# TensorE's reads of expert numbers in the routed loops of layers 1 and 2: four checked reads for a pair of tiles, or one read of three at the head

## The chip, the cores and the metric

The kernel runs on one core of a Trainium2 chip, in one launch. The metric is the device time of that launch in microseconds. Times "from the span's start" count from the first instruction of the profiled execution.
## What is computed

Four transformer layers, each a cross-attention and then a mixture of eight experts, of which every token uses two. Layers 1 and 2 are the ones that the change touches:

```python
# layer 1: 2048 tokens, D = 256, hidden 512, top 2 of 8, and a shared expert
h1 = einsum('td,edh->eth', xf, w1);  h3 = einsum('td,edh->eth', xf, w3)
y  = einsum('eth,ehd->etd', silu(h1) * h3, w2)
out = einsum('etd,te->td', y, cw) + silu(xf @ sw1) * (xf @ sw3) @ sw2
# layer 2: hidden 1024, top 2 of 8
h = gelu(einsum('nd,edf->enf', u, W1) + b1)
out = einsum('ne,end->nd', gates, einsum('enf,efd->end', h, W2) + b2)
```

The kernel computes an expert only for the tokens that chose it.

## The kernel before

**Routing.** The router's choice is turned into a list of slots: tokens that chose the same expert stand together, in tiles of 128 rows. 2048 tokens with two choices each, and up to 7 partly filled tiles, make SLOT_TILES = 39 tiles. VectorE writes two small tables in `vector_tables` (L504): `table`, the expert of each tile, clamped to 7 where it is made (L522), and `rows`, where the tile's rows lie in memory. The tables hold 42 entries of int32 on one partition.

**The routed loop.** `routed_layer` (L1871) is used for layers 1 (swiglu, hidden 512) and 2 (gelu, hidden 1024). All weights of the eight experts are resident in SBUF, so choosing an expert is choosing an address. Each engine has its own program, and `each_pair` (L1945) makes it go over the 39 tiles in pairs: tiles 0 and 1 are written out, then a hardware loop `Fori(1, 19)` runs 18 times with two tiles in its body (2i and 2i + 1, u = 0 and 1), and tile 38 is written out behind it. The loop's own steps (count, compare and branch, copy of the index) are recorded at L1948.

**TensorE's order for tile j** (the body at L2106):

- L2109 and L2110 wait for the rows of tile j + 1 to be in SBUF and for the turned rows of tile j to be copied out; `turn_rows` (L2087, matmuls at L2090) transposes the rows of tile j + 1;
- L2113 and L2114 read from `table` the expert of tile j and that of tile j - 1, each by `expert_of` (L2100, one value a read, with a check of its bounds while running; the records stand at L2101);
- the first product (L2120) of tile j with w1 and w3 of its expert (layer 1), or with two halves of w1 (layer 2): four matmuls of 512 columns, each recorded as two passes, so 8 records a tile;
- the second product (`output`, L2093, matmuls at L2096) of tile j - 1 with w2 of *its* expert: 8 records a tile in layer 1, 16 in layer 2;
- the transposes (L2132) of the hidden values of tile j, which wait (L2128) until they are there.

So four reads are made for a pair of tiles, of three different entries: 2i - 1, 2i (twice) and 2i + 1. After the loop the expert of the last tile is read once more (L2137).

**Around it.** VectorE copies the turned rows to SBUF (L2245), makes the hidden values (layer 1: L2272, silu times the second half; layer 2: it adds the bias at L2267 and ScalarE applies gelu at L2171), copies the output (L2253, L2255) and the turned hidden values (L2277). SyncE loads the rows of tile j + 2 (L1981) and stores the output of tile j - 1 (L2008); in layer 2 it loads bias rows too, and has checked reads of its own (L1963, L1978). None of these programs is touched. The block ends with a barrier of all engines, and the next layer's attention begins behind it.

**The same read elsewhere.** Layer 0's loop (`routed_half_layer`, written out, with no hardware loop) already reads two entries at once, without a check (`experts_of`, L2453, recorded at L2454).

Of the kernel before, what the change touches and what calls it, by code (L numbers as in the profile page):

```python
# [28 lines left out]
E = 8  # L29
# [1841 lines left out]
def routed_layer(nc, kept, cfg, route, resident, w, slots_in, slots_out, pre_next):  # L1871
# [15 lines left out]
    NT = SLOT_TILES  # L1887
    LAST = len(cfg.choose_groups) - 1
    COUNT_AT = D

    ctx = ExitStack()
    with ctx:
# [9 lines left out]
        ident, table = kept.ident, route.table  # L1902
# [42 lines left out]
        def each_pair(engine, body):  # L1945

            body(0, 2)
            with engine.Fori(1, NT // 2) as i:  # L1948
                body(i, 2)
            body(NT // 2, NT % 2)  # L1950
# [80 lines left out]
        @block.tensor  # L2031
        def _(pe):
            def shared_first(n):
                g, m = divmod(n, M)
                if n >= 2:
                    pe.wait_ge(sh_ready, n - 1)
                for bank, weight in zip(banks[2 * (m % 2):2 * (m % 2) + 2], (sw1, sw3)):
                    for k in range(DK):
                        last = nc.tensor.matmul(bank[:, 0:GN], weight[:, k, m * P:(m + 1) * P],
                                                route.xT[:, k, g * GN:(g + 1) * GN], start=(k == 0), stop=(k == DK - 1))  # L2040
                last.then_inc(sh_full, 1)

            def shared_second(g):
                for m in range(M):
                    pe.wait_ge(sh_ready, g * M + m + 1)
                    if m == 0 and g > 0:
                        pe.wait_ge(sy_out, g * GT)
                    for t in range(GT):
                        last = nc.tensor.matmul(banks[4 + t][:, 0:D], shT[:, m, t * P:(t + 1) * P], sw2[:, m, :],
                                                start=(m == 0), stop=(m == M - 1))  # L2050
                        if m == M - 1:
                            last.then_inc(sy_full, 1)

            def shared_expert():
                shared_first(0)
                shared_first(1)
                route.tensor_turn(pe, banks[4], BATCH - 1).then_inc(turned_full, 1)
                shared_first(2)
                pe.wait_ge(turned, 1)
                route.tensor_logits(banks[5], BATCH - 1).then_inc(logits_full, 1)  # L2060
                shared_first(3)
                pe.wait_ge(route.logged, 1)
                shared_second(0)
                shared_first(4)
                shared_first(5)
                pe.wait_ge(sy_out, GT)
                route.tensor_count(pe, count_bank, LAST, COUNT_AT).then_inc(counted, 1)
                shared_first(6)
                shared_first(7)
                pe.wait_ge(count_out, 1)  # L2070
                shared_second(1)
                for g in range(2, NG):
                    for m in range(M):
                        shared_first(g * M + m)
                    shared_second(g)

            if cfg.shared:
                pe.wait_ge(resident.shared_in, 48)
                shared_expert()
                pe.wait_ge(sy_out, TILES)  # L2080
            else:
                route.tensor_count(pe, count_bank, LAST, COUNT_AT).then_inc(counted, 1)
                pe.wait_ge(count_out, 1)
            pe.wait_ge(route.tabled, 1)
            pe.wait_ge(resident.landed, resident.total)

            def turn_rows(u):  # L2087

                for k in range(DK):
                    last = nc.tensor.transpose(a_bank[:, k * P:(k + 1) * P], xg[u][:, k * P:(k + 1) * P], ident[:, :])  # L2090
                last.then_inc(a_full, 1)

            def output(e, u):  # L2093

                for m in range(M):
                    last = nc.tensor.matmul(d_bank[:, 0:D], hT[u][:, m, :], resident.second[:, bass.ds(e, 1), m, :],  # L2096
                                            start=(m == 0), stop=(m == M - 1))
                last.then_inc(d_full, 1)

            def expert_of(j):  # L2100
                return nc.tensor.value_load(table[0:1, bass.ds(j, 1)], min_val=0, max_val=E - 1)  # L2101

            pe.wait_ge(xg_in[0], 16)
            turn_rows(0)

            def body(i, tiles):  # L2106
                for u in range(tiles):
                    j = 2 * i + u
                    pe.wait_ge(xg_in[1 - u], 16 * (i + 1 + u))  # L2109
                    pe.wait_ge(a_out, j + 1)  # L2110
                    turn_rows(1 - u)
                    first = isinstance(i, int) and i + u == 0
                    e = expert_of(j)  # L2113
                    e_before = None if first else expert_of(j - 1)  # L2114
                    pe.wait_ge(h_done, CREDIT + HD * j)
                    for c in range(NB):
                        for k in range(DK):
                            weight = resident.firsts[c if swiglu else 0]
                            cols = slice(0, 512) if swiglu else slice(c * 512, (c + 1) * 512)
                            last = nc.tensor.matmul(b_banks[c][:, :], xgT[u][:, k, :], weight[:, bass.ds(e, 1), k, cols],  # L2120
                                                    start=(k == 0), stop=(k == DK - 1))
                        last.then_inc(b_full, 1)
                    if not first:
                        pe.wait_ge(c_out, CREDIT + HC * j)
                        pe.wait_ge(d_out, CREDIT + j - 1)
                        output(e_before, 1 - u)
                    for c in range(HC):
                        pe.wait_ge(h_done, CREDIT + HD * j + (c + 1 if gelu else 1))  # L2128
                        if c == 0:
                            pe.wait_ge(c_out, CREDIT + HC * j)  # L2130
                        for m in range(4):
                            last = nc.tensor.transpose(c_banks[c][:, m * P:(m + 1) * P],  # L2132
                                                       h[:, (4 * c + m) * P:(4 * c + m + 1) * P], ident[:, :])
                        last.then_inc(c_full, 1)

            each_pair(pe, body)
            e_last = expert_of(NT - 1)  # L2137
            pe.wait_ge(c_out, CREDIT + HC * NT)
            pe.wait_ge(d_out, CREDIT + NT - 1)
            output(e_last, (NT - 1) % 2)  # L2140
# [37 lines left out]
        def _(dve):  # L2178
# [28 lines left out]
            if cfg.shared:  # L2207
# [12 lines left out]
                dve.wait_ge(counted, 1)  # L2220
                route.vector_slots(step, count_bank, LAST, COUNT_AT)
                route.vector_totals(step, count_bank, COUNT_AT)
                dve.sem_inc(count_out, 1)
# [9 lines left out]
            else:  # L2233
                route.vector_ask(dve, step, LAST)
                route.vector_choose(dve, step, LAST)
                dve.wait_ge(counted, 1)
                route.vector_slots(step, count_bank, LAST, COUNT_AT)
                route.vector_totals(step, count_bank, COUNT_AT)
                dve.sem_inc(count_out, 1)
# [736 lines left out]
def build(nc, ap, x_out):  # L2976
# [17 lines left out]
    for n in range(4):  # L2994
        experts, w = EXPERTS[n], weights(f"f{n}_")
        rows_in, rows_out = (half_in, half_out) if n == 0 else (slots_in, slots_out)
        with ExitStack() as held:
# [25 lines left out]
            if n == 0:  # L3023
                routed_half_layer(nc, kept, experts, route, resident, w, rows_in, rows_out, ahead[n + 1], ap["ctx"])
            elif n < 3:
                routed_layer(nc, kept, experts, route, resident, w, rows_in, rows_out, ahead[n + 1])
            else:
                dense_layer(nc, kept, experts, route, resident, x_out, w)
# [17 lines left out]
```

## Time and profile before

| what | us |
|---|---|
| median of 3 runs | 2201.01 (2200.44 to 2202.23) |
| the profiled execution, whole | 2198.09 |
| its span, first to last instruction | 2196.3 |
| around the span | 1.8 |
| layer 1's routed loop, first L2120 of tile 0 to that of tile 38 | 808.40 to 1055.00 |
| layer 2's routed loop, the same | 1271.95 to 1576.17 |
| PE busy over the whole span | 1955.2 (89%) |

### The profile page before, as it was taken

The page shows a single profiled execution, that of the slowest core. Times are in us where ns is not written, and L with a number is a line of the kernel's source. Part 1 is how long each engine was busy: PE and PEld are TensorE (multiplying, and loading weights), DVE is VectorE, ACT ScalarE, POOL GpSimd, SP SyncE. Part 2 cuts the span into 40 slices and gives each one's busy share as a digit, 9 for nine tenths or more (in the row PEclk, how much of TensorE's full clock was granted, in tenths as well). Part 3 has the DMA queues.
Part 4 walks back from the last instruction along what each step waited for, and adds up shares of the span by engine and source line. Part 5 has one row for each costly group of instructions (what it writes and reads, how often), then busy time and mean ns, then how long its engine had stood idle before and what let it go on. Part 6 is the DMA issues. An engine that isn't in the chain of part 4 may idle for free. (4 is left out here: it accounts for less than half of the span.)

```text
span 2196.3 us, 30936 instructions
## 1 busy us (share of the span) xinstructions
PE 1955.2 (89%) x9735; PEld 1309.1 (60%) x9736; DVE 1221.0 (56%) x3287; ACT 710.1 (32%) x1593; POOL 223.8 (10%) x237
## 2 busy tenths in 40 slices
PE   4999889889987999999797389999969999999999
PEld 3666555557765655555575356777635666655665
DVE  3878885557777423333356634444326766667553
ACT  3556652555543100000243211111124444433221
POOL 1000211021011200000411400000060000000000
PEclk8999999999998999999898689999979999999999
DMA  5563103321101311111444234433331000001001
GB/s 166 162 202 125 62 11 108 112 68 59 64 28 53 109 43 41 40 41 41 154 160 139 103 113 115 117 116 115 106 91 30 15 16 15 15 10 29 15 1 39
DMA packets 145523, 167.34 MB, mean 76 GB/s; under 512 B 15225, under 2 KB 124802, under 8 KB 145410
## 3 DMA queue, kind: packets, MB, share of 16 engines
q1 hardware_dynamic: 134754, 142.78, 21.0%
q0 software_dynamic: 8192, 20.98, 3.0%
q10 hardware_dynamic: 2464, 2.10, 0.3%
q8 instruction: 67, 1.10, 0.2%
q14 instruction: 46, 0.38, 0.1%
HBM read 111.03 MB, written 50.59 MB: 74 GB/s over the span
## 5 line engine op out<-in xcount | busy, mean ns | idle before, releaser
L2120 PE MATMUL r_bank<-r_w,r_xgT 128*128 x624 | 288.6, 606 | 16.0 <-issue 14.7
L2096 PE MATMUL r_bank<-r_w,r_hT 128*128 x936 | 214.9, 379 | 1.9 <-DVE r_hT L2277 1.9
L2096 PEld LDWEIGHTS r_bank<-r_w,r_hT 128*128 128x128 f32 x936 | 177.7, 190 | 58.9 <-issue 38.7
L1394 DVE COPY a_probsT<-a_t 128x512 f32<-128x512 f32 x320 | 204.9, 681 | 2.8 <-PE a_t L1035 2.5
L1019 PE MATMUL a_s<-a_kT,a_qT 32*128 32x256 f32 (+2 forms) x1024 | 184.9, 469 | 22.8 <-issue 14.5
L1035 PEld LDWEIGHTS a_t<-kept_ident,a_probs 128*128 128x128 f32 x1280 | 139.9, 143 | 103.2 <-issue 64.5
L1035 PE MATMUL a_t<-kept_ident,a_probs 128*128 128x128 f32 x1280 | 180.2, 283 | 22.0 <-DVE a_probsT L1394 21.1
L2120 PEld LDWEIGHTS r_bank<-r_w,r_xgT 128*128 128x128 f32 x624 | 113.7, 192 | 140.1 <-issue 140.1
L1050 PE MATMUL a_o_bank<-a_probsT,a_v 128*64 128x256 f32 (+1 forms) x1280 | 169.7, 395 | 8.5 <-ACT a_o_raw L1197 7.9
L1167 ACT ACTIVATE a_probs<-a_s,a_negmax 128x512 f32<-128x512 f32 x128 | 86.8, 683 | 160.1 <-DVE a_negmax L1373 160.0
L2171 ACT ACTIVATE r_h<-r_bank 128x512 f32<-128x512 f32 x78 | 46.6, 597 | 283.1 <-DVE r_bank L2267 283.1
L1177 ACT ACTIVATE a_probs<-a_s,a_negmax 128x256 f32<-128x256 f32 x256 | 102.3, 471 | 94.4 <-DVE a_negmax L1377 94.0
L1019 PEld LDWEIGHTS a_s<-a_kT,a_qT 32*128 32x128 f32 (+1 forms) x1024 | 86.8, 188 | 76.3 <-issue 50.0
L1377 DVE CUSTOM_DVE_ANT_0 a_s<-a_s,a_mask_bias 128x256 f32<-128x256 f32 x256 | 101.1, 457 | 40.7 <-PE a_s L1019 39.7
L1050 PEld LDWEIGHTS a_o_bank<-a_probsT,a_v 128*64 128x64 f32 (+1 forms) x1280 | 75.9, 128 | 64.3 <-issue 33.0
L1373 DVE TENSOR_REDUCE a_negmax<-a_s 128x1 f32<-128x512 f32 x128 | 82.3, 684 | 49.2 <-PE a_s L1019 48.4
L959 PE MATMUL a_s<-a_xT,kept_weights 128*128 128x256 f32 x448 | 107.8, 394 | 0.0
L2846 DVE SCALAR_TENSOR_TENSOR kept_x<-d_y,d_gate,kept_x 128x256 f32<-128x256 f32 x144 | 64.3, 483 | 70.7 <-PE d_y L2773 70.7
L2173 ACT ACTIVATE r_silu<-r_bank 128x512 f32<-128x512 f32 x39 | 23.3, 597 | 234.6 <-PE r_bank L2120 234.6
L2272 DVE TENSOR_TENSOR r_h<-r_silu,r_bank 128x512 f32<-128x512 f32 x39 | 26.8, 688 | 129.8 <-PE r_bank L2120 129.8
L959 PEld LDWEIGHTS a_s<-a_xT,kept_weights 128*128 128x128 f32 x448 | 85.2, 195 | 21.1 <-issue 5.1
L555 POOL DMA_INDIRECT slots_in<-f_xn,f_slot x64 | 62.5, 976 | 287.1 <-DVE f_slot L499 268.8
(278 smaller groups left out, 3101.3 us busy)
## 6 DMA issues: line engine op xcount, KB each, us to landing
slots_in<-a_zeros SPq DMA_DIRECT2D x8, 2048.0 KB, 13.7
r_w<-in_f_w SPq DMA_DIRECT2D x16, 1024.0 KB, 7.7
r_w<-in_f_w SPq DMA_DIRECT2D x24, 512.0 KB, 5.3
f_xT<-in_f_b SPq DMA_DIRECT2D x21, 512.0 KB, 3.7
r_xg<-slots_in SPq DMA_DIRECT2D x82, 128.0 KB, 2.0
f_xn<-in_f_b SPq DMA_DIRECT2D x20, 512.0 KB, 3.7
slots_out<-r_y SPq DMA_DIRECT2D x78, 128.0 KB, 1.7
half_in<-a_zeros SPq DMA_DIRECT2D x8, 1024.0 KB, 9.5
```

Of the source, the lines that this page charges most:

```text
L959: last = nc.tensor.matmul(out, weight[:, k, c * P:(c + 1) * P], src[:, k, :], start=(k == 0), stop=(k == DK - 1))
L1019: last = nc.tensor.matmul(out, qT[rows, e % 2, m, c, t * P:(t + 1) * P], kT[rows, e % 2, c, :], start=True, stop=True)
L1035: last = nc.tensor.transpose(bank[:, n * P:(n + 1) * P], src, ident[:, :])
L1050: last = nc.tensor.matmul(o_bank[g * R:(g + 1) * R, 0:SEQ], v[:, e % 2, kt, h, :], probsT[:, half, i, kt, :], start=(kt == 0), stop=(kt == ...
L1167: last = nc.scalar.activation(probs[:, g % PROBS, i, :], bank[:, :], ACT.Exp, bias=negmax[:, g % 4, i, 0:1], accum_out=sums[:, e % 2, t_on ...
L1177: last = nc.scalar.activation(probs[:, g % PROBS, i, cols], bank[:, cols], ACT.Exp, bias=negmax[:, g % 4, i, t:t + 1], scale=-1.0)
L1373: ins = nc.vector.tensor_reduce(negmax[:, g % 4, i, 0:1], s_bank(n)[:, :], AX_X, ALU.max, negate=True)
L1377: ins = nc.vector.tensor_tensor_reduce(out=cols, in0=cols, in1=mask_bias[:, b % 2, t, :], scale=-1.0, scalar=3e38, op0=ALU.add, op1=ALU.mi ...
L1394: nc.vector.tensor_copy(dst, t_bank(n)[:, :].rearrange("p (k n) -> p k n", k=KT)).then_inc(t_free, 1)
L2096: last = nc.tensor.matmul(d_bank[:, 0:D], hT[u][:, m, :], resident.second[:, bass.ds(e, 1), m, :], start=(m == 0), stop=(m == M - 1))
L2120: last = nc.tensor.matmul(b_banks[c][:, :], xgT[u][:, k, :], weight[:, bass.ds(e, 1), k, cols], start=(k == 0), stop=(k == DK - 1))
L2846: nc.vector.scalar_tensor_tensor(out=kept.x[:, tile, :], in0=y_bank[t][:, 0:D], scalar=gate[:, tile, e:e + 1], in1=kept.x[:, tile, :], op0 ...
```

## The change

The four checked reads of a pair give way to one read at the head of the pair's body, ahead of the waits and of `turn_rows`, of the three entries 2i - 1, 2i and 2i + 1, without the check while running (the table is clamped when it is made). For tiles 0 and 1 two entries are read, for tile 38 two (37 and 38), and behind the loop the last one, alone and without a check. Matmuls, their order, waits and all other engines' programs stay.

```diff
-            def expert_of(j):
-                return nc.tensor.value_load(table[0:1, bass.ds(j, 1)], min_val=0, max_val=E - 1)
+            def experts_of(j, n):
+                _, experts = nc.values_load_multi_w_load_instructions(
+                    table[0:1, bass.ds(j, n)], engines=[mybir.EngineType.PE], min_val=0, max_val=E - 1,
+                    skip_runtime_bounds_check_because=CLAMPED)
+                return list(experts)
...
             def body(i, tiles):
+                if isinstance(i, int) and i == 0:
+                    experts = [None] + experts_of(0, tiles)
+                else:
+                    experts = experts_of(2 * i - 1, tiles + 1)
                 for u in range(tiles):
                     j = 2 * i + u
                     pe.wait_ge(xg_in[1 - u], 16 * (i + 1 + u))
                     pe.wait_ge(a_out, j + 1)
                     turn_rows(1 - u)
                     first = isinstance(i, int) and i + u == 0
-                    e = expert_of(j)
-                    e_before = None if first else expert_of(j - 1)
+                    e_before, e = experts[u:u + 2]
                     pe.wait_ge(h_done, CREDIT + HD * j)
...
             each_pair(pe, body)
-            e_last = expert_of(NT - 1)
+            e_last, = experts_of(NT - 1, 1)
```

## Rows read from the trace of the kernel before

**Rows 1.** The page: its span, and TensorE's busy time, share and instructions.
```profile
span 2196.3 us, 30936 instructions
PE 1955.2 (89%) x9735; PEld 1309.1 (60%) x9736; DVE 1221.0 (56%) x3287; ACT 710.1 (32%) x1593; POOL 223.8 (10%) x237
```

**Rows 2.** TensorE's waits: total us, times, longest; layer 1's loop, then layer 2's.
```profile
PE r_bank L2120 <- issue: 13.9, 30, 0.7
...
PE r_bank L2120 <- issue: 0.7, 1, 0.7
```

**Rows 3.** Stretches: us long, busy us of PE, PEld, DVE, ACT, POOL, clock, DMA.
```profile
807.50:850.00 42.50, 38.53 (x130) 21.99 (x131) 12.45 (x24) 3.58 (x6) 0.00 (x0) 0.96 0.23 70
900.00:950.00 50.00, 47.23 (x168) 28.38 (x169) 15.41 (x31) 4.78 (x8) 0.00 (x0) 1.00 0.14 42
1400.00:1450.00 50.00, 50.00 (x216) 35.03 (x215) 22.02 (x40) 7.17 (x12) 0.00 (x0) 1.00 0.38 114
```

**Rows 4.** Timeline, layer 1, into an even tile: start, us, engine, line, [idle <- releaser].
```profile
910.15 0.69 DVE L2272 TENSOR_TENSOR r_h<-r_silu,r_bank 128x512 f32<-128x512 f32 x1 [3.02 <-PE r_bank L2120]
911.46 0.57 PEld L2132 LDWEIGHTS r_bank<-kept_ident,r_h 128*128 128x128 f32 x4
912.00 0.25 PEld L2090 LDWEIGHTS r_bank<-kept_ident,r_xg 128*128 128x128 f32 x2
912.92 0.41 DVE L2245 COPY r_xgT<-r_bank 128x256 f32<-128x256 f32 x1
913.13 0.19 PEld L2120 LDWEIGHTS r_bank<-r_w,r_xgT 128*128 128x128 f32 x1 [0.88 <-issue]
```

**Rows 5.** Timeline, layer 1, into the odd tile before it.
```profile
903.94 0.69 DVE L2272 TENSOR_TENSOR r_h<-r_silu,r_bank 128x512 f32<-128x512 f32 x1 [3.54 <-PE r_bank L2120]
905.79 0.25 PEld L2090 LDWEIGHTS r_bank<-kept_ident,r_xg 128*128 128x128 f32 x2
906.41 0.30 PEld L2120 LDWEIGHTS r_bank<-r_w,r_xgT 128*128 128x128 f32 x2 [0.37 <-issue]
```

**Rows 6.** Line L2101 (the reads) in 910.9 to 913.2, the even boundary: duration, first and last start.
```profile
L2101 PEldq FUSED_REGOPS  x4: 42/101/151, 911.5 to 912.7; - x4
L2101 PEldq TENSOR_LOAD <-f_table x2: 300/303/306, 911.6 to 912.4; - x2
L2101 PEldq SEQ_ASSERT  x2: 18/18/18, 912.2 to 913.0; - x2
```

**Rows 7.** Line L1948 (the loop's own steps) in 910.8 to 911.4.
```profile
L1948 PEldq COMPARE_BRANCH  x1: 208/208/208, 911.0 to 911.0; - x1
L1948 PEldq FUSED_REGOPS  x1: 50/50/50, 911.3 to 911.3; - x1
```

**Rows 8.** Line L2454, layer 0's read of two entries at once.
```profile
L2454 PEldq TENSOR_LOAD <-f_table x20: 530/545/728, 376.2 to 421.9; - x20
```

**Rows 9.** Timeline, layer 2, into an even tile.
```profile
1400.37 0.25 PEld L2090 LDWEIGHTS r_bank<-kept_ident,r_xg 128*128 128x128 f32 x2
...
1400.59 0.30 PEld L2120 LDWEIGHTS r_bank<-r_w,r_xgT 128*128 128x128 f32 x2
```

**Rows 10.** Line L2101 in 1397.7 to 1400.1, the same boundary of layer 2.
```profile
L2101 PEldq TENSOR_LOAD <-f_table x2: 298/302/306, 1398.5 to 1399.2; - x2
L2101 PEldq SEQ_ASSERT  x2: 18/18/18, 1399.0 to 1399.8; - x2
```

**Rows 11.** Timeline: first weight load of tiles 0, 1, 38 (layer 1), 0, 1 (layer 2).
```profile
808.40 0.30 PEld L2120 LDWEIGHTS r_bank<-r_w,r_xgT 128*128 128x128 f32 x2 [0.62 <-issue]
...
816.11 0.30 PEld L2120 LDWEIGHTS r_bank<-r_w,r_xgT 128*128 128x128 f32 x2 [0.89 <-issue]
...
1055.00 0.19 PEld L2120 LDWEIGHTS r_bank<-r_w,r_xgT 128*128 128x128 f32 x1 [0.40 <-issue]
...
1271.95 0.50 PEld L2120 LDWEIGHTS r_bank<-r_w,r_xgT 128*128 128x128 f32 x2 [0.59 <-issue]
...
1280.88 0.30 PEld L2120 LDWEIGHTS r_bank<-r_w,r_xgT 128*128 128x128 f32 x2 [0.92 <-issue]
```

More of the change, by code:

```diff
@@ L1889, in routed_layer @@
     COUNT_AT = D
+    CLAMPED = "the table is clamped to its last entry when it is made"
     ctx = ExitStack()
```

## The prediction, made before the changed kernel ran

> **What bounds the kernel now.** The page comes first: TensorE is busy 89% of the span [rows 1], so the kernel is bound by it in most places, and the question is whether the edited instructions lie where it is *not* busy. Then the list of waits: in layer 1's loop TensorE stands before L2120 for 13.9 us, 30 times, and the reason given is "issue", which means that nothing was handed to it; in layer 2's loop behind tile 0 this happens once, for 0.7 us [rows 2]. So layer 1 has a recurring hole before the first product, layer 2 has none.
>
> The timeline shows the hole from near. Into an even tile, the last operation before it is the pair of row transposes, whose weight loads start at 912.00, and L2120's first weight load starts at 913.13 after 0.88 us of idleness [rows 4]. Into the odd tile it is 905.79 and 906.41, after 0.37 us [rows 5]. How close they could stand is seen in layer 2: 1400.37 and 1400.59, 0.22 us, with no idleness [rows 9]. I measure by the starts of weight loads, since the ends of matmuls are modelled. So an even tile of layer 1 loses 1.13 - 0.22 = 0.91 us and an odd one 0.62 - 0.22 = 0.40 us.
>
> What fills the hole is seen by asking for the line of the reads: in the even one the first register step starts at 911.5, the two loads at 911.6 and 912.4, the last check at 913.0 [rows 6], and L2120 starts at 913.13. And they don't start earlier because the sequencer was held: the hidden values are ready at 910.15 + 0.69 = 910.84 [rows 4], the loop's branch starts at 911.0 and its index step at 911.3 [rows 7], all within a few tenths after it. The transposes L2132 wait for the hidden values and the sequencer passes them only then. It is therefore a chain in layer 1: hidden values ready, loop steps, row transposes handed over, reads, first product.
>
> **Part 1, the reads of the odd tile go.** They start behind the odd tile's hand-over of its row transposes. Without them the sequencer needs only its waits and an address step. The hidden values of that tile are ready at 903.94 + 0.69 = 904.63, the array wants L2120 at 905.79 + 0.22 = 906.01 [rows 5], so 1.38 us are there for a few steps of 0.05 us [rows 7]. The array then sets the time and the whole 0.40 us is gained. What is late next is the array itself.
>
> **Part 2, at the head four steps become one read.** Removed behind the row transposes: two loads of 0.30, two register steps of 0.15 that belong to the checks, two asserts of 0.02, two index steps of 0.05 and the gaps between, from 911.5 to 913.03, together 1.5 us [rows 6]. Added ahead of them: an index step and one load of three values. No row shows a load of three. One value takes 0.30 us [rows 6] and two take 0.545 [rows 8], so the third should add another 0.24: 0.79. The lower bound is 0.55, if the third value were free. The upper bound is three separate loads with an index step each, 3 x 0.36 + 2 x 0.10 = 1.28. I take 0.79, since the rows for one and two are the same operation on the same table.
>
> Where it stands matters: it is now *in front of* the row transposes, which the array was ready for at 912.00. Worked out: the index step of the loop ends at 911.3 + 0.05, the next step can start at 911.36. Index step of the read 0.10 (from 911.5 to 911.6 in rows 6), load 0.79, gap 0.06, wait and hand-over 0.10: the row transposes start at 912.40, 0.40 us later than now. Behind them L2120 follows after 0.22, at 912.62 in place of 913.13. The even tile gains 0.51 us of its 0.91. Queued behind the late row transposes is VectorE's copy of the turned rows (L2245); it starts at 912.92 today, after another copy, and the transposes would be done about then, so at most 0.1 us is added to it; its reader is the first product of the *next* tile, 6 us later. SyncE's next load of rows also waits for these transposes, and its data are wanted a tile later too. Nothing here is near.
>
> **Part 3, the edges of layer 1.** The idleness of the weight loads before L2120 stands in [rows 11]: the gain where the read is hidden is that idleness plus 0.03 (0.88 against 0.91, 0.37 against 0.40). Tile 0: 0.62. I take 0.60: the read of two moves under the copy of the first turned rows, for which TensorE waits anyway. Tile 1: 0.92. Tile 38, behind the loop, with a read of two and no jump back: 0.43. The read behind the loop is followed by a wait for the last copies: nothing.
>
> **Part 4, layer 2.** In the steady state the last check of the even tile ends at 1399.8 [rows 10] and, with the steps behind it, L2120 is handed over at about 1400.1, while the array reaches it at 1400.59 [rows 9]. So the four reads are hidden with 0.5 us to spare, under eight passes of transposes that layer 1 has only half of, and taking them away gives nothing. The read at the head is hidden too: the first read's index step ends at about 1398.4 (the load starts at 1398.5), plus 0.79 and 0.2 for the wait and the hand-over makes 1399.4, and the row transposes are wanted at 1400.37; the cover is 1.0 us. If it were gone, a longer read would count in full in 18 pairs. Only tiles 0 and 1 show the hole: 0.59 and 0.92 [rows 11]. I take 0.50 (its transposes run at the half clock level and are slower) and 0.95.
>
> **The sum.** 18 pairs in layer 1: 18 x (0.51 + 0.40) = 16.4. Edges of layer 1: 0.60 + 0.92 + 0.43 = 1.95. Layer 2: 1.45. Together 19.8 us. The gain reaches the end in full: both loops end in a barrier of all engines, and the next attention starts from that. Against the profiled execution (2198.09, with a span of 2196.3 [rows 1]) that is 2178.3; the median of the runs is 2.9 above that execution, so the forecast is 2201.0 - 19.8 = 2181.2.
>
> A rule that speaks against it. The row shows that the reads of the even tile start 0.7 us behind the hidden values, never ahead of them. The Trainium skill ("Perfetto Trace Analysis", Tensor Engine Instruction) says that a matmul is pushed into a wait queue, that its semaphore wait is spent there, and that the sequencer is free for the next instruction at once. By that rule the reads would be over long before the array needs them and the sum would be 0 in place of 19.8. Here the trace does not agree: the branch at 911.0 follows the 910.84 of VectorE. It is rival B.
>
> **The rivals.**
> - A, the library splits the read of three into three reads. Then the load costs 1.08 to 1.28, the even tile gains 0.51 - 0.39 = 0.12 (middle), and 18 x 0.39 = 7.0 us of the sum go: 2188.2. For it: no row shows a load of more than two. Against it: layer 0's read of two is one instruction (20 loads for 20 pairs) [rows 8]. Chance 0.12.
> - A', the third value costs nothing: even tiles gain 0.24 more, 4.3 us: 2176.9. Chance 0.08.
> - B, the sequencer isn't held at the transposes; the hole has another cause, which stays when the reads go, and the sequencer merely arrives early: 2201. Against it: in layer 2 the reads have the same length and there is no hole, since there is more array work behind the release. The rule of the page in the paragraph above would give this. Chance 0.04.
> - C, slower: the read at the head holds back the row transposes for longer than both removals give. In layer 1 a pair gains 0.91 with a read of 0.79, so it turns to a loss from a read of 0.79 + 0.91 = 1.70 us on; layer 2 begins to lose at 0.79 + 1.0 = 1.8. For it: the index starts at an odd entry, and no row shows that. Against it: the largest single and double loads are 0.31 and 0.73 [rows 6, 8]. At 2.2 us it would cost 18 x (0.50 + 0.4) = 16 us, less 3.4 at the edges: 2214. Chance 0.03.
> - D, the clock. The first stretch of layer 1's loop has a granted clock of 0.96, the 2.4 GHz level with some time at 1.2 GHz [rows 3]; if a smaller hole moves the fall or the rise there or in layer 2's first tile, the time moves by 1 or 2 us either way. It widens the range and is no case of its own.
>
> **How the numbers follow.** Forecast 0.73 (2178.5 to 2184.5, from a load of 0.65 to 0.95), A 0.12, A' 0.08, B 0.04, C 0.03. The range takes in A' and A, as the ends of the one unknown cost: 2176.0 to 2188.5. A measurement of this kernel can tell about 0.2%, 4.4 us, from no change. Faster than that: forecast, A and A', 0.93, of which I put 0.01 aside for a mishap that eats most of it: 0.92. Within 0.2%: B and half of that mishap and a short C, 0.05. Slower: 0.03.
>
> **What would show it.** In the changed kernel's trace: TensorE's wait before L2120 for "issue" in layer 1's loop falls from 13.9 us to under 1 us, and a smaller one before L2090, about 0.3 to 0.4 us each 18 times, comes in its place; one load of three values, 18 times in each loop, with a median near 790 ns; an even tile of layer 1, from L2120 to L2120, goes from 6.72 us (906.41 to 913.13 [rows 4, 5]) to about 6.2, and the odd one loses its 0.37 us of idleness; in layer 2 nothing changes behind tile 1. Wrong would be: three loads a pair (A), a hole before L2120 that stays (B), an even tile longer than 6.72 (C). If the loops shrink by some 20 us and the whole time doesn't, the step on the barrier is wrong.

## The result and the profile after

| | before | changed |
|---|---|---|
| median, 7 runs each | 2201.09 us (2197.83 to 2202.60) | 2185.62 us (2171.03 to 2191.15) |
| ratio, 95% interval | | 0.9917 (0.9888 to 0.9946) |
| profiled execution, whole | 2198.09 | 2176.72 |
| its span | 2196.3 | 2174.9 |
| its granted clock, mean | 0.952 | 0.951 |

The changed kernel is faster by 0.8%. The forecast was 19.8 us less than before: 2178.3 for a profiled execution and 2181.2 for the median. Between the two profiled executions 21.4 us have gone; between the medians 15.5. The executions of the changed kernel lie 20 us apart, those before 5; where that comes from is asked below with traces, since neither of the two traces here shows it.

The page, with the same two lines as in [rows 1]:

```profile
span 2174.9 us, 30438 instructions
PE 1947.7 (90%) x9735; PEld 1307.6 (60%) x9736; DVE 1221.3 (56%) x3287; ACT 710.1 (33%) x1593; POOL 224.0 (10%) x237
```

The matmuls are the same 9735; 498 instructions have gone, all of them sequencer steps. In the stretches (columns as in [rows 3]) the middle one, in layer 1's loop, shows the steady state; the first also has a granted clock of 1.00 where it was 0.96:

```profile
807.50:850.00 42.50, 39.09 (x141) 22.62 (x141) 14.34 (x29) 4.18 (x7) 0.00 (x0) 1.00 0.24 74
900.00:950.00 50.00, 49.49 (x186) 30.24 (x184) 17.68 (x35) 4.78 (x8) 0.00 (x0) 1.00 0.14 45
1400.00:1450.00 50.00, 50.00 (x216) 35.44 (x215) 20.11 (x36) 7.33 (x13) 0.00 (x0) 1.00 0.41 119
```

TensorE is busy 49.49 of 50 us there, where it was 47.23. The list of TensorE's waits from 806 to 1045 us, against the first row of [rows 2] (us in total, times, longest):

```profile
PE r_bank L2091 <- DMA r_xg<-slots_in: 1.2, 1, 1.2
...
PE r_bank L2091 <- issue: 0.2, 1, 0.2
```

The 13.9 us before the first product are gone from the list. (Lines have moved: L2091 is the row transposes, L2127 the first product, L2097 the second, L2139 the transposes of hidden values, L2102 the reads, L2279 VectorE's hidden values.) The timeline into an even tile, against [rows 4]:

```profile
903.93 0.69 DVE L2279 TENSOR_TENSOR r_h<-r_silu,r_bank 128x512 f32<-128x512 f32 x1 [2.63 <-PE r_bank L2127]
...
905.24 0.57 PEld L2139 LDWEIGHTS r_bank<-kept_ident,r_h 128*128 128x128 f32 x4
...
906.18 0.20 PEld L2091 LDWEIGHTS r_bank<-kept_ident,r_xg 128*128 128x128 f32 x2 [0.37 <-issue]
...
906.35 0.30 PEld L2127 LDWEIGHTS r_bank<-r_w,r_xgT 128*128 128x128 f32 x2
```

The hole has moved one step forward: the weight loads of the row transposes now stand idle for 0.37 us, and the first product follows with no idleness. (The list above gives the gaps between matmuls; this hole is read from the weight loads.) From the hidden values' end (903.93 + 0.69 = 904.62) to the first product it is 1.73 us; it was 913.13 - 910.84 = 2.29. The loop's first step of TensorE's sequencer in that boundary:

```profile
L1949 PEldq ALU_OP  x1: 32/32/32, 904.7 to 904.7; - x1
```

It starts 0.06 us after the hidden values are ready. The same 0.06 us stand between the end of VectorE's hidden values and the next step of TensorE's sequencer in each of the 39 tiles of layer 1, in this trace and in that of the kernel before; the step before it lies 2.9 us or more back. So the sequencer was held until then every time.

Into the odd tile, against [rows 5], there is no hole at all:

```profile
911.95 0.25 PEld L2091 LDWEIGHTS r_bank<-kept_ident,r_xg 128*128 128x128 f32 x2
...
912.17 0.30 PEld L2127 LDWEIGHTS r_bank<-r_w,r_xgT 128*128 128x128 f32 x2
```

The reads of layer 1's loop and of layer 2's, where [rows 6, 8, 10] answer (duration in ns: least, median, largest; first and last start):

```profile
L2102 PEldq TENSOR_LOAD <-f_table x21: 311/768/771, 808.9 to 1042.3; - x21
...
L2102 PEldq TENSOR_LOAD <-f_table x21: 313/772/786, 1250.9 to 1559.8; - x21
```

The 21 are one for tiles 0 and 1, 18 in the loop, one for tile 38 and the single one at the end. The 18 are one load of three values each, and it takes 0.77 us. Last the edges, against [rows 11]: tiles 0 and 38 of layer 1, tiles 0 and 1 of layer 2, and a boundary of its steady state, as it was in [rows 9]:

```profile
810.11 0.19 PEld L2127 LDWEIGHTS r_bank<-r_w,r_xgT 128*128 128x128 f32 x1
...
1037.76 0.30 PEld L2127 LDWEIGHTS r_bank<-r_w,r_xgT 128*128 128x128 f32 x2
...
1252.40 0.55 PEld L2127 LDWEIGHTS r_bank<-r_w,r_xgT 128*128 128x128 f32 x2
...
1259.42 0.30 PEld L2127 LDWEIGHTS r_bank<-r_w,r_xgT 128*128 128x128 f32 x2
...
1402.86 0.25 PEld L2091 LDWEIGHTS r_bank<-kept_ident,r_xg 128*128 128x128 f32 x2
1403.08 0.30 PEld L2127 LDWEIGHTS r_bank<-r_w,r_xgT 128*128 128x128 f32 x2
```

By loops, from the first product of tile 0 to that of tile 38: layer 1 took 1055.00 - 808.40 = 246.6 us and takes 1037.76 - 810.11 = 227.7; layer 2 took 304.2 and takes 302.3.

### The profile page after: what moved, and what is told of

The parts are those of the page before. It is cut to its first block and busy times, and to the rows that moved or that the text cites. A ratio compares the mean times of both kernels' runs of the same rounds, so it can differ in the third digit from the quotient of the medians.

```text
span 2174.9 us, 30438 instructions
## 1 busy us (share of the span) xinstructions
PE 1947.7 (90%) x9735; PEld 1307.6 (60%) x9736; DVE 1221.3 (56%) x3287; ACT 710.1 (33%) x1593; POOL 224.0 (10%) x237
## 5 line engine op out<-in xcount | busy, mean ns | idle before, releaser
L2127 PE MATMUL r_bank<-r_w,r_xgT 128*128 x624 | 281.9, 594 | 0.0
L2097 PE MATMUL r_bank<-r_w,r_hT 128*128 x936 | 214.9, 379 | 1.9 <-DVE r_hT L2284 1.9
L2097 PEld LDWEIGHTS r_bank<-r_w,r_hT 128*128 128x128 f32 x936 | 177.7, 190 | 58.9 <-issue 38.7
L1019 PE MATMUL a_s<-a_kT,a_qT 32*128 32x256 f32 (+2 forms) x1024 | 185.8, 471 | 22.7 <-issue 14.5
L1035 PE MATMUL a_t<-kept_ident,a_probs 128*128 128x128 f32 x1280 | 180.5, 284 | 22.8 <-DVE a_probsT L1394 22.6
L2127 PEld LDWEIGHTS r_bank<-r_w,r_xgT 128*128 128x128 f32 x624 | 113.0, 191 | 112.7 <-issue 112.7
L2279 DVE TENSOR_TENSOR r_h<-r_silu,r_bank 128x512 f32<-128x512 f32 x39 | 26.8, 688 | 109.2 <-PE r_bank L2127 109.2
```

Source lines behind the costliest of these rows:

```text
L1019: last = nc.tensor.matmul(out, qT[rows, e % 2, m, c, t * P:(t + 1) * P], kT[rows, e % 2, c, :], start=True, stop=True)
L1035: last = nc.tensor.transpose(bank[:, n * P:(n + 1) * P], src, ident[:, :])
```

## The experiments

A loop's length is again from the first product of tile 0 to that of tile 38, by weight loads, except in the table of stretches further down, which goes to the last record of the first product. The experiments were run on three chips: the two single layers, the unchecked version begun a step earlier and a first repeat of the changed kernel (e1) on one where the kernel before takes 2255.1 us (chip X); the four unchecked single reads, both versions with three checked reads and the kernel before again (e8) on one where it takes 2201.4 (chip Y); the further runs of the changed kernel and of the version begun a step earlier on one where it takes 2254.6 (chip Z). Only ratios and stretches are compared between them.

**Each layer alone.**

```diff
+                at_head = cfg.layer == 1        # e2_layer1; cfg.layer == 2 in e3_layer2
+                if not at_head:
+                    experts = None
...
+                    if at_head:
+                        e_before, e = experts[u:u + 2]
+                    else:
+                        e = expert_of(j)
+                        e_before = None if first else expert_of(j - 1)
```

> Layer 1 alone reads at the head, layer 2 keeps its four checked reads. The sequencer theory: 18.4 us of the loops' gain stay (16.4 in the pairs, 1.95 at the edges), layer 1's even tile at 6.16 us and odd tile at 5.82 as in the changed kernel, layer 2's loop as before (302 to 304 us from tile 0). The rival (the gain comes from all reads alike, so half of it in each layer) expects 10 us.

> Layer 2 alone reads at the head. The sequencer theory: layer 1's tiles stay at 6.72 and 6.21 us, layer 2's stay at 7.98 behind tile 1, and only tiles 0 and 1 gain, 1.5 us in all: the time is that of the kernel before within 0.2%. The rival of equal shares expects 10 us less. If the spread of the changed kernel comes from the shift of what follows layer 1, the times here should lie as close together as those before (within 5 us).

Measured: layer 1 alone 0.9920 (0.9890 to 0.9950), layer 2 alone 1.0006 (0.9990 to 1.0023); the whole change on the same chip, in the same comparison, 0.9915 (0.9892 to 0.9937). In the traces layer 1's loop is 227.8 us with its own change (even tiles 6.16, odd ones 5.82), and with layer 2's alone its tiles stay at 6.7 and 6.2. TensorE's first waits in layer 1's loop, with layer 2's change alone and then with layer 1's alone (the top line of each list):

```profile
PE r_bank L2137 <- issue: 14.3, 30, 1.0
```

```profile
PE r_bank L2091 <- DMA r_xg<-slots_in: 1.2, 1, 1.2
```

The 14 us before the first product (L2137 here) are there in the one and absent in the other. Layer 2's own part is seen in its loop's edge only: the step from tile 0 to tile 1 takes 8.8 us with checked reads and 7.0 with the read at the head. Not all of these 1.8 us are the reads': the granted clock rose 4.4 us behind the first product of tile 0 in the one trace and 2.5 us behind it in the other, and a second trace of the kernel before (e8 below), where it rose after 2.9 us, has 8.08 us there in place of 8.93. So the gain is layer 1's, and equal shares (0.996 each) are excluded. The last sentence expected for layer 2 alone (times within 5 us of each other) missed: its ten lie between 2250.8 and 2262.6, as wide as those of the kernel before on that chip (2249.3 to 2268.3).

**Only the checks are taken away.** The four reads of a pair stay single and where they were.

```diff
             def expert_of(j):
-                return nc.tensor.value_load(table[0:1, bass.ds(j, 1)], min_val=0, max_val=E - 1)
+                _, (e,) = nc.values_load_multi_w_load_instructions(
+                    table[0:1, bass.ds(j, 1)], engines=[mybir.EngineType.PE], min_val=0, max_val=E - 1,
+                    skip_runtime_bounds_check_because="the table is clamped to its last entry when it is made")
+                return e
```

> The kernel before with nothing moved and nothing merged: the same four single reads of a pair, each at its old place behind the row transposes, but without the check while running. Theory K (the checks are the cost): a read falls from 0.67 to 0.36 us; two reads behind the transposes take 0.82 us in the odd tile, which the array covers (tile 5.82), and 0.93 in the even one, after which the first product starts 0.57 us earlier than before (tile 6.15 in place of 6.72). Layer 1's loop from the first product of tile 0 to that of tile 38 is then 229 us, within 2 us of the changed kernel's 227.7, and the ratio to the kernel before is 0.991 to 0.993. Theory M (it is the merging of four reads into one and the place at the head that pay): with four reads left the loop gains less than half, over 237 us, ratio 0.996 or more.

Measured: 0.9918 (0.9888 to 0.9947), the changed kernel's 0.9917 in another place. Layer 1's loop is 1037.49 - 810.31 = 227.2 us, even tiles 6.11 and odd ones 5.81. The reads behind the row transposes of an even tile, and the weight loads of transposes and first product there:

```profile
L2101 PEldq FUSED_REGOPS  x2: 42/46/51, 905.5 to 906.0; - x2
L2101 PEldq TENSOR_LOAD <-f_table x2: 298/304/311, 905.6 to 906.1; - x2
```

```profile
906.04 0.25 PEld L2090 LDWEIGHTS r_bank<-kept_ident,r_xg 128*128 128x128 f32 x2
906.58 0.30 PEld L2123 LDWEIGHTS r_bank<-r_w,r_xgT 128*128 128x128 f32 x2 [0.29 <-issue]
```

Two loads of 0.30 us with a short index step each take 0.9 us together. Here the row transposes are on time and the hole stays before the first product, 0.29 us long; the changed kernel has one of 0.37 us before the transposes. Merging four reads to one and moving it to the head, together, add nothing to the removal of the checks. Theory K holds. No run merges the reads and leaves them behind the row transposes, so what the merging does by itself isn't shown.

**Three checked reads at the head.** This has one read less than the kernel before, all at the changed kernel's place.

```diff
             def experts_of(j, n):
-                _, experts = nc.values_load_multi_w_load_instructions(
-                    table[0:1, bass.ds(j, n)], engines=[mybir.EngineType.PE], min_val=0, max_val=E - 1,
-                    skip_runtime_bounds_check_because=CLAMPED)
-                return list(experts)
+                return [nc.tensor.value_load(table[0:1, bass.ds(j + k, 1)], min_val=0, max_val=E - 1) for k in range(n)]
```

> The changed kernel, but its three entries are read at the head by three single reads with checks (3 x 0.67 and their index steps, about 2.1 us) in place of one read of three (0.77). The sequencer theory: at the head they stand in front of the row transposes, so layer 1's even tile becomes 5.42 + 2.1 = 7.5 us (6.72 before, 6.16 in the changed kernel) and the odd one 5.82; a pair takes 13.3 us against 12.93 before: 7 us slower than before in layer 1's loop although one read of four has gone. In layer 2 the array is reached at 1.75 us of reading, so some 0.3 us a pair, 5 us, are lost there too. Ratio to before 1.002 to 1.006. The rival (fewer reads are always cheaper, wherever they stand) expects 3 of 4 reads to cost three quarters: ratio 0.997 or less.

Measured: 1.0029 (1.0010 to 1.0048), slower by 0.3%. Layer 1's even tiles take 7.50 to 7.56 us and its odd ones 5.82; in layer 2 the even tiles take 8.24 in place of 7.98. The hole is in front of the row transposes:

```profile
899.99 0.57 PEld L2136 LDWEIGHTS r_bank<-kept_ident,r_h 128*128 128x128 f32 x4
902.27 0.20 PEld L2091 LDWEIGHTS r_bank<-kept_ident,r_xg 128*128 128x128 f32 x2 [1.71 <-issue]
902.44 0.30 PEld L2124 LDWEIGHTS r_bank<-r_w,r_xgT 128*128 128x128 f32 x2
```

This is the mechanism of rival C, brought about on purpose, and it has about the size that the rival's thresholds give: for 2.1 us, 0.40 us a pair in layer 1 (measured 0.38) and 0.3 in layer 2 (measured 0.26). What stands at the head counts in full from the point where the array has caught up.

**The same reads, one step earlier in the loop.** The body is begun one step earlier: the transposes of the last hidden values move from the end of a tile's step to the start of the next one's, so the read and the branch come ahead of them. The order of matmuls and waits on TensorE is the same.

```diff
+            def turn_hidden(j):
+                for c in range(HC):
+                    pe.wait_ge(h_done, CREDIT + HD * j + (c + 1 if gelu else 1))
...
             def body(i, tiles):
...
                 for u in range(tiles):
                     j = 2 * i + u
+                    first = isinstance(i, int) and i + u == 0
+                    if not first:
+                        turn_hidden(j - 1)
                     pe.wait_ge(xg_in[1 - u], 16 * (i + 1 + u))
...
                         output(e_before, 1 - u)
-                    for c in range(HC):
...
             each_pair(pe, body)
+            turn_hidden(NT - 1)
```

With the unchecked read of three:

> As the changed kernel, with the body of TensorE's loop begun one step earlier: the read of three and the loop's branch now stand ahead of the transposes of the last hidden values of the pair before, for which the sequencer waits anyway (it is there 3.3 us before they are ready). Order of matmuls and waits is the same. The sequencer theory: the read (0.77 us) and the branch vanish, layer 1's even tile goes from 6.16 to 5.82 us, 18 x 0.34 = 6.1 us less than the changed kernel in the loop; layer 2's loop is unchanged. The rival (the read costs the array something wherever it stands, or the sequencer was not held by the wait) expects no change from the changed kernel.

With three checked single reads:

> The same three checked single reads, in the body begun one step earlier, so that they and the branch stand ahead of the transposes of the hidden values, where the sequencer waits for 3.3 us in layer 1. The sequencer theory: 2.1 us of reads and 0.5 of the loop's steps fit in that wait, so layer 1's tiles are 5.82 us, even and odd, as with the unchecked read of three in that place, and the ratio to before is 0.989 to 0.990, although more is read and checked than in the changed kernel. In layer 2 nothing changes. The rival (the length of the reads decides) expects a time above that of the changed kernel, 0.995 or more.

Measured: unchecked 0.9893 (0.9873 to 0.9912), where the changed kernel has 0.9915 on the same chip; checked 0.9869 (0.9852 to 0.9886), on the chip where the unchecked single reads have 0.9918. In both all tiles of layer 1 behind tile 1 take 5.82 us, and the loop 222.0 and 221.3 us in place of 227.7. The checked one is faster than was expected of it (0.989 to 0.990), and the loops don't explain that: against the kernel before on this chip layer 1's gained 25.3 us and layer 2's lost 0.6, where the medians differ by 29.0. The other 4 us lie outside the loops, and no run shows why. In the checked one, the first two lines lead into an odd tile and the last two into the even tile behind it:

```profile
899.99 0.25 PEld L2091 LDWEIGHTS r_bank<-kept_ident,r_xg 128*128 128x128 f32 x2
900.21 0.30 PEld L2136 LDWEIGHTS r_bank<-r_w,r_xgT 128*128 128x128 f32 x2
...
905.81 0.25 PEld L2091 LDWEIGHTS r_bank<-kept_ident,r_xg 128*128 128x128 f32 x2
906.02 0.30 PEld L2136 LDWEIGHTS r_bank<-r_w,r_xgT 128*128 128x128 f32 x2
```

Three checked reads, 2.1 us, which at the head cost an even tile 0.8 us against the kernel before, cost nothing in the sequencer's wait for the hidden values. They just fit: in the boundary shown the sequencer is through with them and at its wait 0.4 us before the hidden values are ready. The trace of the unchecked one shows the other half, the read itself: 765 ns at 887.8, over 1.9 us before the hidden values are ready (VectorE makes them from 889.75 to 890.44). It is not shorter, it is early.

```profile
L2102 PEldq TENSOR_LOAD <-f_table x1: 765/765/765, 887.8 to 887.8; - x1
```

**Beside the changed kernel.** To compare them again on one chip, and to see where the spread of the changed kernel lies, it was run four times more without an edit, and the kernel before and the version begun a step earlier once more each.

> The changed kernel once more, unedited, since its seven executions lie between 2171 and 2191 us where those before lie between 2198 and 2203. Theory C (clock): both routed loops take the same time in every execution (layer 1 from the first product of tile 0 to that of tile 38 227.7 us, layer 2 302.3 us), and an execution near 2188 has its extra 10 us in layer 2's attention, where the granted clock in the profiled execution changed between its two levels many times; its mean granted clock is 0.945 in place of 0.951. Theory L (loop): the extra time lies in the routed loops, whose reads or loads differ from run to run; then the loops of a slow trace are longer. Both expect times between 2171 and 2191 again, ratio 0.988 to 0.996.

> The kernel before, unedited, for a trace on this chip, to see by stretches where its time goes in another execution. If the spread of both kernels lies in the attention of layers 0 to 2 and in the granted clock there, the two routed loops take 249.7 and 307.3 us here as in the first trace (within 2 us for a fall of the clock in them), and the difference of the spans lies between the loops.

> The changed kernel again, for a second and third set of times and for traces of single executions. Its times on the first chip fell into two groups, 2171 to 2178 with a mean granted clock of 0.951 and 2186 to 2191 with 0.945. The trace of the unchecked reads (2191, 0.943) has the routed loops as fast as in the first group, but its dense layer of layer 3 takes 136.3 us from the first to the last hidden product in place of 130.5, with the granted clock at half in two places there, and the attention of layer 2 3 us more. Theory C (clock, outside the loops): a trace of about 2188 of this kernel shows the same, dense layer near 136 us and loops at 230.7 and 305.2; one of about 2176 shows 130.5. Theory L expects the extra time in the loops.

> As the one before: the same kernel, one more execution with a trace. Theory C: loops at 230.7 and 305.2 us whatever the whole time is; what varies is the granted clock in layer 2's attention and in the dense layer.

> As the one before, a third execution with a trace, with the same expectation.

> The body begun one step earlier with the unchecked read of three, beside the changed kernel on the same chip: 5 to 6 us less than it where the clock falls at the same places (a pair 11.63 in place of 11.98 us, 18 pairs, and layer 1's loop at 225.0 in place of 230.7). The rival, that the hidden read gains nothing at the end, expects equal times.

Measured: the changed kernel 0.9915 (0.9892 to 0.9937, chip X) and 0.9909 (0.9880 to 0.9938) of the kernel before, the one begun a step earlier 0.9876 (0.9843 to 0.9910), 2228.5 us against 2236.3. The intervals of the two overlap, so the medians alone don't tell them apart; the loop does (224.5 against 231.0 us to the last record of the first product). With its checked twin it has the lowest ratios here. The times of the changed kernel, expected between 2171 and 2191 us again, came out at 2230 to 2248 on chips X and Z, where the kernel before takes 54 us more too. The kernel before on chip Y has the span of its first trace (2196.4 and 2196.3), so there was no difference to look for.

The stretches of five traces of the changed kernel (us; "loop" to the start of the last record of the first product, "attention 2" between the loops, "dense" the hidden products of layer 3, "tail" behind the last of them), and of two of the kernel before:

| trace | span | loop 1 | attention 2 | loop 2 | dense | tail |
|---|---|---|---|---|---|---|
| before, first trace | 2196.3 | 249.7 | 213.8 | 307.3 | 130.5 | 14.5 |
| before, e8 (chip Y) | 2196.4 | 249.7 | 215.6 | 306.5 | 130.5 | 14.5 |
| changed, first trace | 2174.9 | 230.7 | 211.7 | 305.2 | 130.5 | 14.5 |
| changed, e1 (chip X) | 2233.3 | 231.1 | 241.8 | 305.2 | 130.5 | 14.5 |
| changed, e10 (chip Z) | 2231.8 | 232.3 | 239.4 | 305.3 | 130.5 | 14.5 |
| changed, e9 (chip Z) | 2245.9 | 231.0 | 242.0 | 305.1 | 136.2 | 17.6 |
| changed, e11 (chip Z) | 2243.8 | 232.8 | 239.2 | 305.2 | 134.9 | 20.5 |

The loops of each kernel are the same within 1 us in all (232 to 233 where the clock fell once, at 841 us in e10 and at 842 in e11), on all chips. e9 and e11 are 12 to 14 us longer than e10 on the same chip, and 9 to 10 of it are in the dense layer (5.7 and 4.4) and its tail (3.1 and 6.0). The stretches of the dense layer and of the tail, e9 and then e10:

```profile
2092.00:2228.00 136.00, 135.59 (x459) 85.30 (x460) 65.89 (x166) 30.67 (x45) 0.00 (x0) 0.96 0.04 14
2229.00:2245.00 16.00, 12.99 (x33) 5.75 (x32) 3.87 (x8) 0.69 (x1) 0.00 (x0) 0.71 0.19 66
```

```profile
2087.00:2217.00 130.00, 129.59 (x459) 82.86 (x459) 65.72 (x166) 30.67 (x45) 0.00 (x0) 1.00 0.04 13
2218.00:2231.00 13.00, 9.93 (x32) 4.55 (x32) 3.88 (x8) 0.63 (x1) 0.00 (x0) 0.96 0.27 91
```

The same 459 matmuls take 5.7 us more at a mean granted clock of 0.96 in place of 1.00, with TensorE busy throughout in both. So theory C holds in what matters, the spread on one chip lies outside the loops and goes with the clock, but it named the wrong stage first: layer 2's attention differs by 28 to 30 us between the first trace and chips X and Z, and by at most 3 us between executions on one chip.

## Why the prediction was right, point by point

- **What bounds it.** The hole before the first product was the sequencer's, in layer 1 alone. The two single-layer kernels split the gain as 0.9920 and 1.0006. Right.
- **Part 1, odd tiles.** Forecast 0.40 us each, to the array's own 5.81; measured 6.22 to 5.82. Right.
- **Part 2, the read of three.** Forecast 0.79 us from the rows for one and two values; measured 0.77. The start of the row transposes was forecast at 1.56 us behind the hidden values (912.40 - 910.84) and measured at 906.18 - 904.62 = 1.56. That it agrees so well is luck: the read needed no index step of its own and started 0.54 us behind the hidden values, where 0.62 was forecast, and from its end to the row transposes it took 0.25 us, where 0.16 was. The even tile's gain was forecast at 0.51 and measured at 0.56 (6.72 to 6.16); what is left is that the first product follows the row transposes by 0.17 us (906.35 - 906.18) and not by 0.22. The pairs gave 18 x 0.96 = 17.3 us where 16.4 were forecast.
- **Part 2, which of its parts pays.** The prediction summed checks, merging and place as one. The experiment without checks shows that removing the checks alone is worth as much (227.2 us against 227.7 for the loop). By an estimate from these traces, merging saves some 0.1 us of sequencer time in a pair's even tile (two loads and index steps, 0.9, against 0.77), and the place at the head costs it again, by holding the row transposes; no run separates the two.
- **Part 3, edges of layer 1.** Forecast 1.95. Measured: the loop lost 18.9 us and tile 0's own 0.62 us of idleness has gone, 19.5 in all, so 2.2 for the edges. Two things in it are not in the forecast's 1.95, and they are of opposite sign. The granted clock, which fell in tile 0 before (0.96 in that stretch, 1.00 now), gave back up to 1.7 us. Rival D allowed for that, but the change alone doesn't decide it: e10 and e11, of the changed kernel too, have such a fall one tile later, and their loops are 1 to 2 us longer. And the row transposes of tile 1 now wait 1.2 us for the rows of tile 2. In SyncE's queue the load of these rows stands behind eight loads of the next attention's weights; it was issued at 813.03, and the weight loads of the transposes stood idle for 1.4 us, until 816.41. The statement "nothing here is near" was true of the steady state and not of tile 1.
- **Part 4, layer 2.** Nothing in the steady state (7.98 before and after, e3: 1.0006), as forecast. Edges: forecast 1.45, measured 1.9 in the loop and 0.6 in tile 0, 2.5; about 1.0 of it is the clock, which rose sooner in tile 0 (1252.40 to 1259.42 is 7.02 us, 8.93 before, of which the reads explain 0.95). The second trace of the kernel before bears that out: with an earlier rise it has 8.08 us there, 1.06 more than the changed kernel.
- **The sum.** 17.3 + 2.2 + 2.5 = 22.0 in the loops, 21.4 in the span; forecast 19.8. The loops' gain reached the end, as the barriers said. The small difference is itself a sum: the changed trace comes to layer 1's loop some 2.3 us later (its granted clock is 0.51 from 248 to 255 us, where it was 1.00 before), and its attention of layer 2 is 1.5 us shorter. None of that was forecast.
- **The median.** 2185.6, 4.4 us above the forecast, although the profiled execution is 1.6 below its own. Four of the seven executions lie at 2185 to 2191 with a mean granted clock of 0.944 to 0.946, three at 2171 to 2178 with 0.951 and 0.952. The step that failed is the addition of a constant 2.9 us for "median above the profiled one", taken from a kernel whose runs happened to lie close together. The range of 2176.0 to 2188.5 came from the price of the load alone and had no term for this spread; three of the seven executions lie outside it, so that the median lies inside owes something to luck. The 0.2% that a measurement was said to tell was too fine as well: the interval is 0.3% to either side. No trace was taken of the four executions at 2185 to 2191; that they lost their time in the dense layer is inferred from e9 and e11.
- **The rivals.** A and A' fell with one load of 0.77 us a pair. B fell with the times, and the sequencer's wait at the transposes was shown from the other side: reads put ahead of it cost nothing, even 2.1 us of them. C did not occur with this read, but its mechanism did with a longer one, at the size expected for it (tile of 7.5 us, 1.003).

The rule in "Perfetto Trace Analysis" of the Trainium skill (Tensor Engine Instruction), that the sequencer is free again as soon as a matmul is pushed to the wait queue, does not fit these traces for the transposes here: nothing of the next tile's sequencer work starts before the hidden values are there. It starts 0.06 us behind them in all 39 tiles of layer 1, before and after the change.

## What to carry to other kernels

## What the runs showed of the hardware

- A read of table entries by TensorE's sequencer takes 0.30 us for one, 0.545 for two and 0.77 for three values in one instruction, 0.23 us for each more; its check while running adds 0.28 us (from a load's end to the next index step 0.34 us with it, at 911.94 of the kernel before, and 0.06 without, at 905.95 of the unchecked reads; 0.15 of it is a register step and 0.02 the assert).
- TensorE's sequencer does nothing behind a transpose that waits for VectorE until the data are there: its next step starts 0.06 us after VectorE's end in all 39 tiles of layer 1, in the first traces of both kernels. Reads placed ahead of that transpose cost 0 (tiles of 5.82 us), the same reads behind it 1.7 us in an even tile (7.51).
- The granted clock fell to 0.96 in the mean of a stretch in which TensorE was busy 135.6 of 136 us, and stayed at 1.00 in the same stretch of another execution of the same kernel on the same chip. In the first of them (e9) it was at half, the 1.2 GHz level, from 2212.8 to 2219.6 us, with TensorE busy 6.8 of these 6.8 us and all of the 22.8 us before. It cost 4 to 6 us there and 3 to 6 in the tail. What decides it is open; of the fourteen traces of all kernels three show it in the dense layer (the unchecked reads, whose dense layer took 136.3 us, e9 and e11), and a fourth, the checked reads at the head, in the tail alone (18.2 us).
- The same program took 54 us longer on two of the three chips (2255.1 and 2254.6 against 2201.4); of the changed kernel's 58 us between its first trace and e1, 30 lie in layer 2's attention (211.7 and 241.8), where the granted clock was 0.74 in the mean in place of 0.78 and the transfers ran at 131 GB/s in place of 148 (windows 1066 to 1307 us and 1041 to 1252), and 24 ahead of layer 1's loop. The loops took the same time on all. Why is open; no run was made for it.
